# Attention with V as the stationary operand and turned reciprocals, routing by matched maxima, and the gate between the halves of the projection, in a fused attention and expert kernel

## What is computed

```python
x = x + xattn(_layernorm(x), ctx_768, Wq, Wk, Wv, Wo, bo)
x = x + ffn(_layernorm(x), ...)
# xattn: 4 heads of 64
attn = jax.nn.softmax(einsum('bhqd,bhkd->bhqk', qh, kh) * 64 ** -0.5)
ctx = einsum('bhqk,bhkd->bhqd', attn, vh); return ctx @ Wo.T + bo
# ffn: 32 experts in 8 groups of 4
scores = softmax(xf @ gw + gb)
group_scores = sum(top_k(scores by group, 2)); keep the 4 best groups
indices = top_k(scores of the kept groups, 4); weights = scores at indices
y = sum over chosen experts of weight * ((silu(xf@w1e+b1e) * (xf@w3e+b3e)) @ w2e + b2e)
z = (silu(xf@sw1+sb1) * (xf@sw3+sb3)) @ sw2 + sb2; return y + z
```

## Time and profile before

| | us |
|---|---|
| median of 3 runs | 395.49 (395.03 to 395.94) |
| the profiled execution | 394.26 |
| its span in the trace | 392.5 |
| PE busy | 332.1 (85%) |
| DVE busy | 268.4 (68%) |
| ACT busy | 184.0 (47%) |
| POOL busy | 167.7 (43%) |

### The profile page before, as it was taken

How to read it: one execution, slowest core, us unless ns; L and a number is a source line. 1 busy time by engine, 2 the same in 40 slices (tenths; PEclk the granted TensorE clock), 3 DMA queues, 4 the chain that set the end, 5 groups by cost and what they waited for, 6 DMA issues and landing times.

```text
span 392.5 us, 9872 instructions
## 1 busy us (share of the span) xinstructions
PE 332.1 (85%) x2356; PEld 284.5 (72%) x2357; DVE 268.4 (68%) x910; ACT 184.0 (47%) x622; POOL 167.7 (43%) x202
## 2 busy tenths in 40 slices
PE   3999999999999989997999999989898989895000
PEld 2698888888898968785876988778787878684000
DVE  4588597877878696989574565665675645664585
ACT  2486675757567564345112654544545545443000
POOL 4703005352536263556241255555565454555300
PEclk9999999999999999999699999999999999999555
DMA  6897718475612721202314455455555554554898
GB/s 162 287 384 285 241 27 298 149 251 170 210 67 103 290 103 48 88 33 100 115 67 128 118 170 165 150 175 169 155 164 162 163 170 139 176 163 170 328 385 296
DMA packets 33766, 68.96 MB, mean 176 GB/s; under 512 B 5323, under 2 KB 26092, under 8 KB 32076
## 3 DMA queue, kind: packets, MB, share of 16 engines
q1 hardware_dynamic: 26348, 46.95, 37.3%
q0 software_dynamic: 6960, 21.11, 14.7%
q10 hardware_dynamic: 432, 0.59, 0.6%
HBM read 39.87 MB, written 28.77 MB: 175 GB/s over the span
## 4 chain that ended last, share of the span: by engine, by line
PE 41%; DVE 17%; issue 15%; DMA 9%; SPq 7%; ACT 5%; another core or an unknown queue 1%; ACTq 1%; POOL 1%; DVEq 1%; POOLq 0%
PE psS L1166 6%; PE psF L961 5%; DMA xn2T_all<-dispatch 4%; PE psS L1155 4%; PE psS L93 3%; DVE nmax L1232 3%; PE psF L1175 3%; SPq L483 3%; PE psF L1166 3%; SPq L123 2%; DMA w<-shares 2%; PE psF L93 2%; PE psG L1000 2%; PE psS L940 2%; PE psF L1065 1%
## 5 line engine op out<-in xcount | busy, mean ns | idle before, releaser
L657 POOL DMA_INDIRECT shares<-xn2T_all,e_number x81 | 81.1, 1001 | 77.5 <-PE psF L1175 43.3
L614 POOL DMA_INDIRECT dispatch<-work,slot_now x64 | 62.6, 978 | 96.9 <-issue 45.4
L1166 PE MATMUL psS<-work,arena 128*128 128x128 f32 x432 | 57.1, 275 | 0.0
L1166 PEld LDWEIGHTS psS<-work,arena 128*128 128x128 f32 x432 | 52.6, 192 | 0.1
L861 ACT ACTIVATE work<-psS 128x256 f32<-128x256 f32 x81 | 30.9, 383 | 34.9 <-PE psS L1155 20.4
L1626 DVE SCALAR_TENSOR_TENSOR work<-psS,b,work 128x128 f32<-128x128 f32 x54 | 18.8, 349 | 38.8 <-ACT work L872 30.4
L1155 PE MATMUL psS<-ident,xn2T_all 128*128 128x128 f32 x162 | 32.0, 280 | 9.0 <-issue 6.6
L1155 PEld LDWEIGHTS psS<-ident,xn2T_all 128*128 128x128 f32 x162 | 20.6, 141 | 23.5 <-issue 12.5
L1629 DVE COPY arena<-w 128x512 f32 x81 | 35.9, 444 | 2.0 <-issue 2.0
L1175 PE MATMUL psF<-w,work 128*128 x108 | 32.9, 387 | 2.7 <-issue 2.5
L872 ACT ACTIVATE work<-psS,b 128x128 f32<-128x128 f32 x54 | 19.9, 368 | 30.3 <-PE psS L1166 22.0
(11 more groups left out here) (227 smaller groups left out, 794.9 us busy)
## 6 DMA issues: line engine op xcount, KB each, us to landing
xn2T_all<-dispatch SPq DMA_DIRECT2D x81, 160.0 KB
w<-in_w SPq DMA_DIRECT2D x6, 1536.0 KB
w<-shares SPq DMA_DIRECT2D x6, 1024.0 KB, 7.0
dispatch<-padding SPq DMA_DIRECT2D x8, 640.0 KB
w<-in_w SPq DMA_DIRECT2D x1, 2304.0 KB
x<-in_x SPq DMA_DIRECT2D x1, 1536.0 KB, 7.2
w<-shares SPq DMA_DIRECT2D x3, 512.0 KB, 10.9
out<-x SPq DMA_DIRECT2D x3, 512.0 KB, 3.7
```

The source lines that it names most:

```text
L614: pool.indirect_dma_start(dispatch, bass.IndirectOffsetOnAxis(ap=slot_now[:, par, j * TOPK + k:j * TOPK + k + 1], axis=0), xn2[:, par, j, ...
L657: pool.indirect_dma_start(shares, bass.IndirectOffsetOnAxis(ap=e_number[:, u:u + 1], axis=0), e_y[:, u, :], None).then_inc(added[u], 16)
L1166: ins = pe.matmul(hidden_bank(u)[:, m * P:(m + 1) * P], e_w13k[:, u % UNROLL, k, m * INTER:(m + 1) * INTER], e_xT[:, u % 3, k, :], start=( ...
```

## The change

**attend** makes V the stationary operand: for each k (half of the 256 columns), t and r, V's 64 columns of one head are loaded and the turned probabilities of both halves j, 256 columns, stream past. The two heads of a k go to rows 0 to 63 and 64 to 127 of the same bank. That is 8 matmuls in a step, and the result is already turned, so `attend_T` and its copy on ACT go. The softmax sums now lie along the wrong axis: DVE writes the reciprocals (`prcp`), POOL spreads them to 256 columns (`widen`, 2 copies), PE turns them (`shares_T`, 4 transposes), ACT copies them out (`turned_out`), and one DVE operation multiplies (`divide`, 128 x 512), where two of 128 x 256 stood.

**Routing** keeps the exponentials undivided until the weights. Group scores are the maximum over the six pair sums of a group. The top four groups and the top four experts are found with MAX8 and marked with MATCH_REPLACE; `chosen` is then one comparison. One-hot rows, indices and their sort are gone. The rows are the maxima of rows times `chosen`. For the plane numbers PE turns `chosen` (2 matmuls in `ranks`), ACT copies it out (`chosen_out`), and `rank_index` multiplies it with a table (4 matmuls), apart from `ranks` and after it.

**Order.** `gate(b-1)` lies between the halves of `project(b)`; `scores(b+1, 0)` ahead of `rank_index`; `probs_T(b, 0)` ahead of `proj_v`; `norm_T(b+2)` ahead of `shares_T`. `exps(b+1)` is split around `gate_exps(b-1)`. In the last step `silu(1, ·)` comes after `gate_exps` and the three roundings. On POOL the steps are written out, with other events as pace.

```diff
+                pool.wait_ge(s["prcp_ready"], b + 1)
+                if b >= 1:
+                    pool.wait_ge(s["turned_psum"], b)
+                for j in range(TPB):
+                    ins = pool.tensor_copy(wide[:, j], spread(prcp[:, j, :].rearrange("p (r k) -> p k r", k=KD), 3, HD))
+                ins.then_inc(s["wide_ready"], 1)
...
+            def step(b, par, front, front2, tail, tail2, nth=None):
+                first = isinstance(b, int) and b == 0
                 if front:
                     q_out(b + 1)
                     k_out(b + 1)
+                probs_out(b, 0)
+                if front2 and not first:
+                    norm(b + 2)
+                if tail2:
+                    chosen_out(b - 2)
+                if front:
                     v_out(b + 1, 1 - par)
-                probs_out(b, 0)
                 probs_out(b, 1)
+                if front2:
+                    round_context(b + 2, par, nth)
+                if first:
+                    act.wait_ge(s["norm1"], 3)
+                    norm(b + 2)
+                if front2:
+                    norm_out(b + 2)
+                if not front:
+                    silu(0, 0)
+                    silu(0, 1)
+                turned_out(b)
                 if tail:
                     norm2_out(b - 1)
-                if front2:
-                    round_context(b + 2, par, nth)
+                if front:
+                    exps(b + 1, 0)
                 if tail:
                     gate_exps(b - 1)
                     norm2_keep(b - 1)
...
+                if front:
+                    exps(b + 1, 1)
+                else:
                     for c in range(WHOLE, 6):
                         round_chunk(c)
-                    silu(0, 0)
-                    silu(0, 1)
-                attend_out(b)
-                if not front:
                     silu(1, 0)
                     silu(1, 1)
...
+            def shares_T(b, front):
...
+                    pe.wait_ge(s["v_ready"], b + 2)
+                for k in range(KD):
+                    for j in range(TPB):
+                        ins = pe.transpose(shares_bank(b)[:, k * LQ + j * P:k * LQ + (j + 1) * P],
...
+                pe.wait_ge(s["pT_ready"], TPB * (b + 1))
                 pe.wait_ge(s["v_ready"], b + 1)
                 if front:
-                    pe.wait_ge(s["q_ready" if j == 0 else "k_ready"], b + 2)
-                elif j == 1:
...
-                for hp in range(HEADS):
-                    h = (hp % 2) * 2 + hp // 2
+                for k in range(KD):
+                    y = psF[:, 1, k * LQ:(k + 1) * LQ].rearrange("p (j q) -> p j q", j=TPB)
                     for t in range(2):
-                        ins = pe.matmul(psF[:, 2 - j, h * HD:(h + 1) * HD], pT[:, j, t, hp, :], v_sb[:, par, t, h * HD:(h + 1) * HD],
-                                        start=(t == 0), stop=(t == 1))
-                ins.then_inc(s["att_psum"], 1)
...
+            def project(b, front, j):
                 pe.wait_ge(s["attT_ready"], b + 1)
-                if isinstance(b, int) and b == 0:
+                if front and j == 0:
...
                 pe.matmul(psG[:, 64:96], ones[:, :], chosen[:, 1, :], start=False, stop=True)
+                for j in range(TPB):
+                    ins = pe.matmul(psF[0:EXPERTS, 2, j * P:(j + 1) * P], chosen[:, j, :], same[:, :], start=True, stop=True)
...
+            def rank_index(b):
...
+                pe.matmul(index, same[:, :], token_parts[:, 0:1].to_broadcast([P, TPB * EXPERTS]), start=True, stop=False)
+                pe.matmul(index, same[:, :], spread(token_parts[:, ds(TPB * b + 1, TPB)], 2, EXPERTS), start=False, stop=False)
+                pe.wait_ge(s["chosenT_ready"], b + 1)
+                for j in range(TPB):
...
                 if front:
                     proj_q(b + 1)
                     proj_k(b + 1, 1 - par)
+                probs_T(b, 0)
                 if front:
                     proj_v(b + 1, 1 - par)
-                probs_T(b, 0)
-                if not front:
+                else:
                     pe.wait_ge(s["x1_ready"], TPB * (b - 1) + 1)
                     shared_up(0, 0)
-                if tail2 and front:
+                if tail2:
                     ranks(b - 2)
...
+                if front:
+                    scores(b + 1, 0)
+                if tail2:
+                    rank_index(b - 2)
                 if not front:
                     pe.wait_ge(s["pT_ready"], TPB * b + 1)
                     shared_up(0, 1)
-                    ranks(b - 2)
+                if front2:
+                    norm_T(b + 2)
+                shares_T(b, front)
+                attend(b, par, front)
                 if tail:
                     norm2_T(b - 1, 1 - par)
-                attend(b, 0, par, front)
-                if tail:
-                    gate(b - 1)
-                attend(b, 1, par, front)
-                if front:
-                    scores(b + 1, 0)
-                else:
-                    shared_up(1, 0)
-                attend_T(b, front)
                 if front:
                     scores(b + 1, 1)
                 else:
+                    shared_up(1, 0)
                     shared_up(1, 1)
-                if front2:
-                    norm_T(b + 2)
-                project(b)
+                project(b, front, 0)
+                if tail:
...
+                dve.wait_ge(s["probs_ready"], TPB * (b + 1))
+                dve.reciprocal(prcp[:, :, :], psums[:, :, :]).then_inc(s["prcp_ready"], 1)
...
+                dve.wait_ge(s["turned_ready"], b + 1)
+                dve.wait_ge(s["attT_psum"], b + 1)
+                dve.tensor_tensor(attT, psF[:, 1, :].rearrange("p (k q) -> p k q", k=KD), turned,
+                                  ALU.mult).then_inc(s["attT_ready"], 1)
...
+            def route_pairs(b):
...
-                st.need("sorted")
+                e = gexp[:, :, :].rearrange("p t (g c) -> p (t g) c", c=GSIZE)
+                dve.tensor_tensor(pairs[:, :, 0:3], e[:, :, 0:3], e[:, :, 1:4], ALU.add)
+                dve.tensor_tensor(pairs[:, :, 3:5], e[:, :, 0:2], e[:, :, 2:4], ALU.add)
+                st.did(dve.tensor_tensor(pairs[:, :, 5:6], e[:, :, 0:1], e[:, :, 3:4], ALU.add), "pairs")
+                dve.reciprocal(grcp[:, :], gsum[:, :])
+            def route_groups():
+                st.need("pairs")
+                st.did(dve.tensor_reduce(gsum2[:, :, 0:GROUPS], pairs[:, :, :].rearrange("p (t g) c -> p t g c", t=TPB), X, ALU.max), "groups")
...
+            def route_keep():
+                st.need_apart("group order", s["consts"])
+                for j in range(TPB):
+                    ins = dve.match_replace(gkept[:, j, :], gtop[:, j, 0:8], gsum2[:, j, :], MARK)
+                st.did(ins, "groups kept")
...
+            def route_mark():
+                st.need_apart("best", s["consts"])
+                for j in range(TPB):
+                    ins = dve.match_replace(marked[:, j, :], top[:, j, 0:8], masked[:, j, :], MARK)
+                st.did(ins, "marked")
...
+                st.need("marked")
                 with nc.allow_low_precision("zeros and ones"):
...
+                    ins = dve.tensor_scalar(chosen[:, :, :], marked[:, :, 0:EXPERTS], MARK, None, ALU.is_ge)
+                ins.then_inc(s["chosen_ready"], 1)
...
+            def route_weights(b, par):
+                dve.wait_ge(s["chosen_ready"], b + 1)
+                for j in range(TPB):
+                    dve.scalar_tensor_tensor(xn2[:, par, j, D:D + EXPERTS], masked[:, j, 0:EXPERTS], grcp[:, j:j + 1], chosen[:, j, :], ALU.mult, ALU.mult)
...
+                st.did(dve.tensor_tensor(rows_own[:, :, :], rowof[:, :, :], chosen[:, :, :], ALU.mult), "rows own")
...
+            def norm2(b, par, tail, attended=True):
...
                     dve.bn_stats(st2[:, j, :], rows_of(b, j)).then_inc(stats_ready[j], 1)
                 if tail:
-                    route_others(b - 1)
+                    route_pairs(b - 1)
+                    route_groups()
+                    route_top_groups()
+                    route_keep()
+                    route_mask()
...
-                    route_best(b - 1)
...
                 rsqrt_var(n, mv2[:, :, 1])
                 if tail:
...
+                    newton_root(n, tmp)
                 if tail:
-                    route_number()
...
+                    rank_rows(b - 1)
                 newton_wy(n, tmp)
...
+                    rank_base(1 - par)
...
-                newton_root(n, tmp)
+                    rank_top()
...
-                newton_wy(n, tmp)
```

More of the change, by code:

```diff
@@ L79, in need, with need_apart @@
         self.eng.wait_ge(self.sem, self.count(name))
+    def need_apart(self, name, other):
+        nth = self.count(name)
+        if not isinstance(nth, int):
+            nth = self.eng.snap(self.eng.to_reg(nth), min_val=1)
+        self.eng.wait_ge(other, 1)
```

(22 more changed lines are left out.)

406 lines of the change are left out of this document (162 added, 244 removed).

## The result

The change made the kernel **slower: 412.06 us** median (409.31 to 413.91) against 395.3, a ratio of 1.042 (95% interval 1.036 to 1.048). The forecast was 387.5. The profiled execution of the changed kernel took 409.31 us, its span is 407.6.

What follows compares the result with a forecast made beforehand. PE's attention chain, with a short loop through DVE, was taken to bound the kernel. Savings of 11.0 + 1.6 - 0.7 + 2.3 - 5.5 - 0.7 = 8.0 us took 395.5 to 387.5 us, range 381 to 397.

Steps and rivals of the forecast that it cites:

- What bounds the kernel: Attention stage: PE's own work sets the pace, with a short loop through DVE; time spared on PE reaches the end.
- attend, saved 1.60 us a step: Attention step: eight matmuls running in pairs take 1.94 us where the old halves took 3.54; bounds 0.1 and 1.8.
- The rival in which column halves don't run together: In attend: matmuls run one after another, 3.5 us in each of eight steps, 400.3 us in all; chance 0.13.
- The wait of norm2_T: Attention steps: chosen comes about 1 us earlier and norm2_T later, so PE's wait goes; 0.6 us a step saved.
- Turns: Attention step: shares_T saves 0.16 us against attend_T, ranks and rank_index are charged 0.15; net nothing.
- Step 0: First attention step: norm_T(2) comes earlier and PE waits 2.3 us for the norm; 1.6 - 2.3 = -0.7 us.
- Step 7: Last attention step: 3.7 us saved in attend and waits, less 1.4 us of ranks waiting for chosen; 2.3 us saved.
- The last silu: End of attention: silu(1, ·) late in ACT's queue leaves PE idle for 5.5 us before the first shared_down.
- POOL's new copies: Rival, attention steps: widen's copies stop DVE uncovered, 4.8 us lost, 392.3 us; chance 0.16 shared with a second lower-clock stretch.
- The stop goes: Rival, shared expert: the old stop of all engines falls where nobody needs DVE, giving 381.8 us; chance 0.14.
- the second stretch at the lower clock: Shared expert, after the old stop: may cost up to 3.4 us, taken as 0; as a rival it gives 390.9 us.
- The slower side: Whole kernel: the outcome slower than before, chance 0.15, of which 0.13 for column halves that don't run together.

Runs made afterwards that it cites:

- e1: The changed kernel with the scatter's DMA pairs paced over the step in steps 2 to 6, and scatter(6) paced in the shared expert: 397.99 us.
- e3: The changed kernel with the scatter paced and both silu(1, ·) and the first copy of weights ahead of gate_exps in the last step: 389.3 us, ratio 0.987.
- e5: The changed kernel with scatter paced, silu ahead of gate_exps, and the gate put back ahead of both halves of the projection: 380.56 us, ratio 0.967.
- e2: The changed kernel with silu(1, ·) and the first copy of weights ahead of gate_exps in the last step of attention: 401.33 us.
- e12: The changed kernel with the scatter paced and the gate ahead of both projection halves, silu left behind gate_exps and the roundings: 388.65 us, ratio 0.987.
- e7: The kernel before with one edit, the eight indirect DMAs of scatter(6) in the shared expert paced by later events: 389.22 us, ratio 0.990.
- e6: The changed kernel with silu ahead of gate_exps, its own scatter pacing, and a small POOL memset after each indirect DMA of the scatter: 397.39 us.
- e11: The kernel before with its scatter in steps 2 to 7 let go in two groups of four indirect DMAs: 392.81 us, ratio 1.000.
- e4: The kernel before without the waits that pace the scatter in steps 2 to 7, eight indirect DMAs back to back: 434.11 us, ratio 1.100.

## Why the prediction was wrong

**What bounds the kernel, "a chain on PE with a short loop through DVE, and what PE is spared there comes off its end"** is the step that failed. The loop has a link that I took to cost nothing: the way of PE's semaphore to DVE, ACT and POOL. The change moved POOL's pace, and the sum has no term for it. I named the new events and asked only what `widen` would do, not what the DMAs would do when their waits had passed. Cost: e1 puts it at 14 us. Two more terms were mis-sized: the order of silu (below), and the gate between the halves of the projection, which stood in the sum at nothing and costs some 8 us once the scatter is paced (e3 and e5).

**attend, saved 1.60 us a step: right.** 1.88 us for eight matmuls against 1.94 forecast, in steps 1 to 7; in the first step, at the lower clock, they take 3.3. The rival in which column halves don't run together fell at once. The Trainium skill, "TensorEngine Tiling (Array Packing)", Key Properties: tiles operate independently. The trace agrees, 0.235 us a matmul where one alone takes 0.43.

**The wait of norm2_T: right**, none in steps 1 to 7. **Turns: right**, `shares_T` 0.53 to its successor.

**Step 0: right for the wait**, 2.32 us against 2.3, partly by luck: the sum's 27.98 + 1.1 is 29.1 and not 29.3, as the trace has it (29.08), and PE came 0.2 us earlier than counted. That 3.4 us at the lower clock follow was not in the sum. **Step 7:** `ranks` waited 4.0 us and not 1.4, since `chosen` hangs on a residual that was late; with the scatter paced it is 1.7 (e1).

**The last silu: right in size and place (5.54 us against 5.5), too small in what follows.** I counted 5.5 us and no further loss of clock. e2 and e12 price the order at 10.7 and some 8: the stretch at the lower clock was 13.7 us, not 6.8.

**POOL's new copies.** DVE's operations beside `widen` do take longer, 0.42 and 0.29 us where 0.16 is usual, but DVE waits for `ranks` behind them, as the sum said, if 0.81 us and not 1.4. DVE and POOL at 93 us:

```profile
93.29 0.42 DVE L1262 TENSOR_SCALAR rsq<-rsq 128x2 int32<-128x2 int32 x1
93.75 0.29 DVE L1266 TENSOR_TENSOR rstd<-rsq 128x2 f32<-128x2 f32 x1
94.08 0.16 DVE L1270 SCALAR_TENSOR_TENSOR rstd<-rstd,rsq 128x2 f32<-128x2 f32 x1
```

```profile
93.29 0.75 POOL L632 COPY w<-prcp 128x256 f32<-128x256 f32 x2 [1.88 <-DVE prcp L1286]
```

The Trainium skill, "SBUF — State Buffer", Who interferes with whom (an exclusive lock), agrees in kind: here it costs 0.4 us a step, all covered.

**The stop goes:** it didn't. PE waits 2.2 us at 193.09, ahead of it stands a run of six DMAs (183.94 to 191.32), and the second stretch at the lower clock follows, whose 3.4 us the sum had left to the range. The cause was read wrongly, too. I put it beside POOL's subtraction, which ended at the same time; e7 shows that it was the run of eight DMAs ahead of it.

**The slower side had a wrong mechanism.** It stood at 0.15 and rested on the column halves. That a wait on POOL may be what keeps POOL from doing harm was not among the rivals.

With the scatter paced and silu and the gate moved forward (e5), the change gives 380.56 where the kernel before with its own run of eight paced gives 389.22, in the same group of runs: 8.7 us less. So a gain of the expected size was there, hidden behind the change's order. It isn't shown to be that of V stationary and matched routing alone, since neither silu nor the gate stands in e5 where the kernel before had it.

**Open:** how the DMAs hold back semaphores. In the trace's events, increments by the DMAs' own landings are late in the same way (those of the fourth and fifth DMA of the run above come mostly with the sixth's, at 126.1 to 126.3 us), while those of DVE and ACT are on time (within 0.01 us). It isn't a load of weights beside the scatter: from 116 to 130 us the only DMA traffic is that of POOL's own queue. Whether distance or number decides is not settled (e6 didn't change the distance), nor is there a length of run at which the delay begins: it is 0.6 us behind four DMAs in e11, 2.5 us in the kernel before, and what it costs depends on who waits. Nor is it shown by what path the gate's place gains its 8 us with the scatter paced.

## What to carry to other kernels

A wait that seems to cost nothing on an engine that isn't the bottleneck may be a pace: before an edit moves the events that indirect DMAs wait for, count how many will go out in one run and what other engines' semaphores fall beside it. Where an engine gets a semaphore later than the work behind it ended, look at all engines at that time before blaming one of them. In a hand-written queue, put what the next stage waits for ahead of work that is needed later.

## What the runs showed of the hardware

- Six indirect DMAs on POOL, 1.27 us apart, delay semaphores of PE by up to 3.6 us in the changed kernel, eight by 3.4 to 6.5 us in e4; four with a pause behind them still delay one by 0.6 us (e11), without cost. Semaphores of DVE and ACT are on time beside them.
- PE at the lower clock for 13.7 us after an idle time of 5.5 us (and of 4.6 in e12), for 6.8 us after 2.2 and 2.3, for 3.4 us after 2.3 in the first step: the 5.5 us of idle time cost some 6.8 us more (an estimate, half of 13.7).
- Two fp32 matmuls of 64 columns of weights in different column halves run beside each other: 1.88 us for eight, 0.235 each, where one alone takes 0.43.
